# Two-layer decoder kernel: routing work of the last attention spread over four groups, range clears of semaphores, and two loads moved to GpSimd's queue

## The reference, cut to what matters

```python
x = ln(x + attn0(x)); x = ln(x + xattn0(x, ctx)); x = ln(x + soft_moe(x))
x = ln(x + attn1(x)); x = ln(x + xattn1(x, ctx)); x = ln(x + block(x))
def block(x):                                   # the last stage, with an attention of its own
    x = x + attention(layernorm(x, ln1_g, ln1_b))          # causal, 16 heads
    flat = layernorm(x, ln2_g, ln2_b)                      # 2048 tokens, 256 wide
    logits = flat @ gate_W + gate_b                        # 8 experts
    top_v, top_i = top_k(logits, 2); w = softmax(top_v)
    return x + sum over the 2 chosen experts e of w_e * (gelu(flat @ W1[e] + b1[e]) @ W2[e] + b2[e])
```

## Time and profile before

| | us |
|---|---|
| median of 3 runs (2824.33 to 2837.35) | 2835.46 |
| the profiled execution | 2807.25 |
| its span | 2805.4 |
| PE busy | 2516.5 (90%) |
| DVE busy | 1493.9 (53%) |
| ACT busy | 1326.3 (47%) |
| POOL busy | 452.0 (16%) |

### The profile page before, as it was taken

One profiled execution on the slowest core, in us unless ns is written; L12 is line 12 of the kernel. 1 busy time (PEld: TensorE's weight loads), 2 busy tenths in 40 slices (PEclk: granted clock), 3 DMA queues, 4 the chain that ended last, 5 costly groups with the idle time before them and its releaser, 6 DMA issues. The chain is left out here.

```text
span 2805.4 us, 47501 instructions
## 1 busy us (share of the span) xinstructions
PE 2516.5 (90%) x15751; PEld 1441.7 (51%) x15752; DVE 1493.9 (53%) x4204; ACT 1326.3 (47%) x2826; POOL 452.0 (16%) x730
## 2 busy tenths in 40 slices
PE   6999999999979889999699999999998998499991
PEld 3555544444434456676365544444445555267761
DVE  2555777788644500023455588878756565222224
ACT  3655466677754421111255556766675444122220
POOL 4233212101100000000113322112122123200004
PEclk8999999999999999999799999999999888699995
DMA  7555534232700022103644452332322445211103
GB/s 226 159 141 145 134 96 104 53 80 69 251 1 1 1 96 95 65 21 138 180 133 140 138 131 66 83 102 67 101 76 80 136 144 197 74 32 32 34 30 96
DMA packets 158432, 276.79 MB, mean 99 GB/s; under 512 B 22928, under 2 KB 101008, under 8 KB 153744
## 3 DMA queue, kind: packets, MB, share of 16 engines
q1 hardware_dynamic: 155152, 265.71, 33.1%
q0 software_dynamic: 3072, 8.39, 0.9%
HBM read 195.51 MB, written 95.29 MB: 104 GB/s over the span
## 5 line engine op out<-in xcount | busy, mean ns | idle before, releaser
L1626 ACT ACTIVATE second_p<-psum 128x512 f32<-128x512 f32 (+3 forms) x1024 | 462.2, 521 | 262.0 <-PE psum L1427 258.4
L1626 ACT ACTIVATE first_p<-psum 128x512 f32<-128x512 f32 (+3 forms) x768 | 366.6, 549 | 166.0 <-PE psum L1427 162.6
L1724 DVE TENSOR_REDUCE second_max_parts<-psum 128x1 f32<-128x512 f32 x512 | 322.5, 682 | 67.1 <-PE psum L1404 63.7
L1724 DVE TENSOR_REDUCE first_max_parts<-psum 128x1 f32<-128x512 f32 x512 | 322.5, 682 | 64.9 <-PE psum L1404 63.6
L1720 DVE CUSTOM_DVE_ANT_0 second_masked<-psum,mask_qk 128x384 f32<-128x384 f32 (+3 forms) x512 | 229.4, 488 | 196.4 <-PE psum L1404 173.9
L1439 PE MATMUL psum<-second_p,second_v_aug 128*32 128x512 f32 (+3 forms) x2048 | 237.9, 537 | 5.7 <-ACT second_p L1626 4.8
L1417 PE MATMUL psum<-second_q,second_k 64*128 64x512 f32 (+3 forms) x1024 | 226.5, 438 | 9.7 <-DVE second_max_parts L1720 6.8
L1404 PE MATMUL psum<-second_k,second_q 64*128 64x512 f32 (+3 forms) x1024 | 200.8, 389 | 26.3 <-DMA second_k<-a_k_parts 13.7
L1427 PE MATMUL psum<-second_shift_T,choose 64*128 64x512 f32 (+3 forms) x1024 | 199.5, 384 | 0.0
L1417 PEld LDWEIGHTS psum<-second_q,second_k 64*128 64x128 f32 x1024 | 98.5, 188 | 190.6 <-ACT second_p L1626 76.3
L1439 PE MATMUL psum<-first_p,first_v_aug 128*32 128x512 f32 (+3 forms) x1536 | 185.4, 554 | 1.1 <-ACT first_p L1626 0.7
(11 more groups left out here) (339 smaller groups left out, 3740.1 us busy)
## 6 DMA issues: line engine op xcount, KB each, us to landing
first_k<-c_k_parts SPq DMA_DIRECT2D x64, 256.0 KB, 4.8
second_q<-a_q_parts SPq DMA_DIRECT2D x128, 128.0 KB, 2.9
second_k<-a_k_parts SPq DMA_DIRECT2D x128, 128.0 KB, 2.9
second_k<-c_k_parts SPq DMA_DIRECT2D x64, 256.0 KB, 4.9
first_q<-a_q_parts SPq DMA_DIRECT2D x64, 128.0 KB, 3.2
first_k<-a_k_parts SPq DMA_DIRECT2D x64, 128.0 KB, 3.2
c_k_parts<-first_held SPq DMA_DIRECT2D x16, 512.0 KB, 3.2
first_q<-c_q_parts SPq DMA_DIRECT2D x64, 128.0 KB, 4.2
```

The lines of the kernel that those rows point to most:

```text
L1626: evacuated(act.activation(probs[tile % 2][:, 2 * h + p, q0:SEQ], bank[:, q0:SEQ], ACT.Exp, scale=scale), event)
L1724: evacuated(v.reduce_max(max_parts[n % 2][:, h, p, qt, k0 // BANK:k0 // BANK + 1], bank[:, 0:width], axis=AX_X), event)
```

## The change

Four edits:

1. `Core.stage` sorts the numbers of the stage's semaphores and clears each run of consecutive numbers with one instruction.
2. The routing pieces of a2. They are cut finer (`gate_scale` and `gate_add` a tile at a time, `gate_top` in four parts, `gate_place` in three), and for b = 0 and 1 they lie in four groups in place of three: in group first+1 only the output and the statistics; in first+2 aggregate, root, a pause and scale; in first+3 add, a pause, turn, a pause and logits; in first+4 top, a pause and rank; in first+5 place and send. For b = 2 everything ends in group 47 as before, with the rows in 46 and logits to send in 47. For b = 3 it all comes behind the last group, as before.
3. The four gate loads leave the "weights" event and come in a new event at the start of group 4.
4. In the routed stage the down bias and the residual are issued by POOL; the residual only when DVE has read two results. DVE waits for the down bias at the first result.

```diff
                 @block.gpsimd
                 def _(pool):
-                    for sem in self.stage_sems:
-                        pool.sem_clear(sem)
+                    numbers = sorted(sem.num for sem in self.stage_sems)
+                    for _, run in itertools.groupby(enumerate(numbers), lambda x: x[1] - x[0]):
+                        run = [number for _, number in run]
+                        pool.sem_clear(range(run[0], run[-1] + 1))
...
-        pieces += [("gate_stats", slot, 1), ("gate_aggregate", slot, 0), ("gate_root", slot, 0), ("gate_scale", slot, 0)]
+        pieces += [("gate_stats", slot, 1)]
...
+    measure = [("gate_aggregate", slot, 0), ("gate_root", slot, 0)]
+    scale = [("gate_scale", slot, t) for t in range(QT)]
+    add = [("gate_add", slot, t) for t in range(QT)]
+    turn = [("gate_turn", slot, k) for k in range(DK)]
+    top = [("gate_top", slot, part) for part in range(4)]
+    place = [("gate_place", slot, part) for part in range(3)] + [("gate_send", slot, 0)]
+    return measure, scale, add, turn, [("gate_logits", slot, 0)], top, [("gate_rank", slot, 0)], place
...
-                        if gate:
-                            fetch_weights(gate_loads, gate_in)
+                    elif event[0] == "gate_weights":
+                        fetch_weights(gate_loads, gate_in)
...
                 load(tile_at(0, 0, 0))
...
-                sp.dma_start(down_bias[:, :, :].rearrange("p e d -> p (e d)"),
-                             a["L1_ffn_exp_b2"].rearrange("e d -> (e d)").partition_broadcast(P)).then_inc(down_bias_in, 16)
-                for b in range(BATCH):
-                    sp.dma_start(residual[:, b * QT:(b + 1) * QT, :], block_in[b].rearrange("(q p) d -> p q d", p=P)
-                                 ).then_inc(residual_in, 16)
...
                         e = weights_of(v, t)
+                        v.wait_ge(down_bias_in, 16)
...
-                v.wait_ge(down_bias_in, 16)
                 for_steps(v, body)
...
             @block.gpsimd
             def _(pool):
+                pool.dma_start(down_bias[:, :, :].rearrange("p e d -> p (e d)"),
+                               a["L1_ffn_exp_b2"].rearrange("e d -> (e d)").partition_broadcast(P)).then_inc(down_bias_in, 16)
+                pool.wait_ge(y_read, 2)
+                for b in range(BATCH):
+                    pool.dma_start(residual[:, b * QT:(b + 1) * QT, :], block_in[b].rearrange("(q p) d -> p q d", p=P)
+                                   ).then_inc(residual_in, 16)
                 pool.wait_ge(residual_in, 16 * BATCH)
...
-            turned, best, ranked, placed = gate_pieces(slot)
-            if b < BATCH - 1:
+            measure, scale, add, turn, logits, top, rank, place = gate_pieces(slot)
+            if b < BATCH - 2:
                 pieces[first + 1] = pieces.get(first + 1, []) + output_pieces(a2, slot)
-                pieces[first + 2] = [REST] + turned
-                pieces[first + 3] = best + [REST] + ranked + [REST] + placed
+                pieces[first + 2] = measure + [REST] + scale
+                pieces[first + 3] = add + [REST] + turn + [REST] + logits
+                pieces[first + 4] = top + [REST] + rank
+                pieces[first + 5] = place
+            elif b < BATCH - 1:
+                pieces[first + 1] = pieces.get(first + 1, []) + output_pieces(a2, slot) + measure
+                pieces[first + 2] = scale + [REST] + add + [REST] + turn
+                pieces[first + 3] = logits + top + [REST] + rank + place
             else:
-                pieces[first] = output_pieces(a2, slot) + turned + best + ranked + placed
+                pieces[first] = output_pieces(a2, slot) + measure + scale + add + turn + logits + top + rank + place
+        contexts[GROUPS] = [("gate_weights", 0, 0)]
```

More of the change, by code:

```diff
@@ L14 @@
+import itertools
 import math
@@ L1877, in gate_scale, with gate_add @@
                     wait_for(v, gate_sent, 16 * 2 * QT * b)
[L1878 to L1882, removed]
+                    gate_do(v.scalar_tensor_tensor(rows[:, t, :], x_of(slot)[:, t, :], g_mean_var[:, t, 0:1], gate_gain[:, :],
+                                                   ALU.subtract, ALU.mult), wait=t == QT - 1)
+                def gate_add(event):
+                    _, slot, t = event
                     b = slot % BATCH
-                    if b == BATCH - 1:
+                    if b < BATCH - 1:
+                        v.wait_ge(gate_inverted, b + 1)
+                    elif t == 0:
                         v.wait_ge(gate_rooted, 1)
                         gate_do(v.reciprocal(g_rstd[:, :], g_root[:, :]))
[L1887 to L1891, removed]
+                    v.scalar_tensor_tensor(rows[:, t, :], rows[:, t, :], g_rstd[:, t:t + 1], gate_shift[:, :],
+                                           ALU.mult, ALU.add).then_inc(gate_rows, 1)
                 def logits_read(event):
@@ L1905, in gate_top @@
                 def gate_top(event):
-                    _, slot, _ = event
+                    _, slot, part = event
                     b = slot % BATCH
                     tiles = slice(b * QT, (b + 1) * QT)
[L1909 to L1927, removed]
+                    if part == 0:
+                        wait_evacuated(v, ("gate_logits", slot, 0))
+                        for t in range(QT):
+                            gate_do(v.max(top[:, t, :], logits[:, t, :]), wait=t == QT - 1)
+                    elif part == 1:
+                        for t in range(QT):
+                            gate_do(v.max_index(top_at[:, t, :], top[:, t, :], logits[:, t, :]), wait=t == QT - 1)
+                    elif part == 2:
+                        gate_do(v.tensor_tensor(lead[:, tiles], top[:, :, 1], top[:, :, 0], ALU.subtract), wait=False)
+                        gate_do(v.tensor_copy(top_f[:, :, :], top_at[:, :, :]))
+                        v.wait_ge(gate_numbers, NUMBERS)
+                        for x in range(2):
+                            gate_do(v.tensor_tensor(pick[x][:, tiles, :], number[:, 0:E].unsqueeze(1).to_broadcast([P, QT, E]),
+                                                    top_f[:, :, x:x + 1].to_broadcast([P, QT, E]), ALU.is_equal), wait=x == 1)
+                    else:
+                        gate_do(v.tensor_tensor(both[:, tiles, :], pick[0][:, tiles, :], pick[1][:, tiles, :], ALU.add))
+                        for t in range(b * QT, (b + 1) * QT):
+                            ins = v.tensor_tensor(earlier[:, t + 1, :], earlier[:, t, :], both[:, t, :], ALU.add)
+                            if t == (b + 1) * QT - 1:
+                                ins.then_inc(gate_masked, 1)
+                                v.wait_ge(gate_masked, b + 1)
+                            else:
+                                gate_do(ins)
@@ L1929, in gate_place @@
                 def gate_place(event):
-                    _, slot, _ = event
+                    _, slot, x = event
                     b = slot % BATCH
                     tiles = slice(b * QT, (b + 1) * QT)
-                    wait_evacuated(v, ("gate_rank", slot, 0))
-                    for x in range(2):
+                    if x < 2:
+                        wait_evacuated(v, ("gate_rank", slot, 0))
                         gate_do(v.tensor_tensor(picked[:, :, :], pick[x][:, tiles, :], rank_at[:, :, :], ALU.mult))
```

12 lines of the change are left out of this document (6 added, 6 removed).

## The result

The changed kernel takes 2784.7 us (median of 4, 2784.1 to 2791.9) against 2833.6 before: ratio 0.984, interval 0.982 to 0.985. The forecast was 2793. The profiled execution is the one of 2784.09, with a span of 2782.3; that of before took 2807.25. So the two profiled executions lie 23 us apart and the medians 49, and a good part of what follows is about this difference.

What follows compares the result with a forecast made beforehand. PE, busy 90% of the span, was taken as the bound, with time lost to its waits, low clock and stage ends. 13.6 + 19.6 + 1.9 + 7.5 - 0.5 = 42.1 us off the 2835.46 median gave 2793 us, range 2780 to 2808.

Steps and rivals of the forecast that it cites:

- clears: Stage ends: 172 fewer clear instructions at 0.079 us each, all on the path; 13.6 us gained, bounds 0 and 13.6.
- a2: Head groups with routing pieces: fewer waits and the clock staying up; 19.6 us gained, bounds 5 and 28.
- context: Start of "second": the context's load issued earlier, ahead of four gate loads; 1.9 us gained, bounds 0 and 3.
- routed start: Routed stage: tile 1's load issued earlier, so the first up product starts earlier; 7.5 us gained, bounds 5 and 9.
- residual: Routed stage: the residual's 2 MB come while tiles 2 to 4 run; 0.5 us lost, bounds 0 and 8.
- sum: Whole kernel: gains at stage ends, head groups, context and routed start less the residual's loss; 42.1 us gained.
- rival 2: Stage ends: a range clear costs per semaphore, so nothing is gained there; time 2807 us, chance 0.08.
- the prediction's own signs: Wrong if PEclk stays under 0.9 in groups 38 to 44, stage ends take 3 us, or PE waits for row loads.
- rival 1: Head groups: waits move and the clock falls all the same; 4.3 us gained instead of 19.6, time 2808, chance 0.15.
- Queues: Gate loads, down bias and residual moved: 1.9 at the context, 7.5 at the routed start, 0.5 lost to the residual.
- rival 3: Routed stage: row loads land behind the residual, 2.7 us late for three tiles, 8 us; time 2801, chance 0.06.
- the prediction's signs of being wrong: PEclk under 0.9 in groups 38 to 44, stage ends of 3 us, PE waiting for row loads of tiles 2 to 5.

Runs made afterwards that it cites:

- e10: Changed kernel with the logits product of b = 0 and 1 in two halves of 8 matmuls, in groups 39/40 and 43/44; 2788.8 us, 0.9841 of before.
- e8: Changed kernel with routing pieces of b = 0 and 1 set by step, logits halved, rank a step behind top, residual loads two tiles apart; 2789.9 us, 0.9847 of before.
- e6: Changed kernel without the sends of b = 0 and 1, their rows not written; 2771.8 us, 0.9860 of before.
- e4: Changed kernel with place and the eight sends of b = 0 and 1 at the end of groups 40 and 44; 2773.4 us, 0.9865 of before.
- e7: Changed kernel with scale, add, transposes and halved logits of b = 0 and 1 set by hand into their group's four steps; 2782.1 us, 0.9890 of before.

## Why the forecast came out near, step by step

| step | forecast | measured |
|---|---|---|
| clears | 13.6 | 11.9 in the traces, 11.6 alone |
| a2 | 19.6 | 27 with stops; about 15 without |
| context | 1.9 | 2.6 in the first two traces; about 1.7 over all |
| routed start | 7.5 | 6.2 (14.85 to 8.70) |
| residual | -0.5 | -1.0 and -2.4 |
| sum | 42.1 | 49 with stops |

**Clears.** The mechanism was right and rival 2 fell: a range costs by the instruction, with a little by its length (90 ns in the middle, 289 for 48). The price was 0.074 and not 0.079, and the ten new ones cost 1.4.

**a2.** Groups 38 and 42 near 12, 39 and 43 near 17 (16.95, 15.37), the longest unit wait 1.5 and none for the add: all as forecast. Wrong was that the clock stays up. Behind the wait of 1.55 for the unit in group 39 came 3.4 us of 1.2 GHz. The same wait of 1.55 stands in group 43, and no low clock follows it there (15.37 us at 0.98), so the wait alone doesn't decide it. And 40 and 44, which I took at little over the plain 11.56, take 14.02 at 0.79. That fall stands behind no wait but behind the logits product, 1.95 us of sixteen matmuls 8 columns wide. Where the product is cut in halves the clock stays up: groups 40 and 44 are at 1.00 and 1.00 in e10, at 1.00 and 0.97 in e8. How long the fall lasts isn't explained by this: it is 6.8 us in the changed kernel, but 3.4 in e6, with the same product in the same place (group 40 takes 12.65 us there). By the prediction's own signs this part was wrong: PEclk is under 0.9 in groups 39, 40, 41 and 44. So rival 1 was right in its "falls all the same" and wrong in its size: falls of 3.4 and 6.8 us cost 1.6 and 2.5, where groups 38 and 42 lost 9.1 and 10.1 before. Without stops groups 32 to 47 take 257.5 before and 241.6 in e4, 15.9, less 1.2 behind group 47 (43.6 to 44.8 us from there to the clears, of which I had 1): about 15 instead of 19.6, or 17 if the scatter of group 36 is left out. With stops they go from 290.2 to 257.9, 32 us, less 2.4 behind group 47; alone the pieces brought 27, and the other 3 us are not followed up.

The Trainium skill, "TensorE: Matmul & The Clock Gate", section "A second HAM failure mode: psum-queue depth-cycling", lets the clock swing on small idle times. The trace agrees in part: the wait of 1.55 us is followed by low clock in group 39 and not in group 43, and the fall at the start of group 40 stands behind no idle time.

**Queues.** 1.9 + 7.5 - 0.5 = 8.9 forecast, 9 measured (6 to 12), so this sum is right within the interval only; the first two traces give 2.6 + 6.2 - 2.4 = 6.4. PE's wait for the context fell from 9.19 to 6.60 us there, but it scatters: 8.3 to 9.3 in the four traces with the old order of loads, 6.1 to 9.2 in the ten with the new one, 8.9 and 7.2 on average. The routed start gained 1.3 less than forecast: tile 0's transposes began 5.1 us after the issue of its load and tile 1's 4.8 us after theirs, where I had 3.5 for the landing beside the down bias. The 2 MB of residual did delay row loads (one landed after 6.4 us instead of 2.0), as rival 3 said, but for two tiles and by 2.4 us at most. That PE waits for the row load of tile 4 is the second of the prediction's signs of being wrong that came. The rule of "DMA: Bandwidth & Descriptors", section "Queues, rings and completion order" in the Trainium skill, that a semaphore waits for its engine's earlier writes in all queues, agrees with that 6.4.

**The step that failed** is the one ahead of the sum: "The median of the runs shown lies 28 us above that execution, for no reason that the trace can show; taken off the median the forecast is 2793". There was a reason, and it touched the change: by their times most executions had stops beside the very sends that it moves (only the profiled ones can be looked into). The change took away some of their price: groups 40, 41, 44 and 45 together take 82.1 us in the second trace of before and 79.5 in the changed kernel's first, though the new ones hold the top and rank besides, and 46 and 47 fell from 30.2 to 19.6. That the forecast landed within 9 us is luck in part: the sum of 42.1 was made for a kernel without stops, where e4 gained 38 (0.9865 of 2811), and was taken off a median with stops, where the gain was 49. It lies between the two since a2 was forecast 3 to 5 us too high for the first case. Against its own kind, taken off the 2811.2 of the set without stops, the forecast would have been 2769; e4 took 2773.

## What to carry to other kernels

When the profiled execution lies a per cent under the median, as here, the trace may show another case than the times: ask for a second trace before a sum is taken off the median. Look for low clock behind work too, and not only behind waits: the product 8 columns wide was followed by it here, and its halves with other work between them were not. Laying DVE's work into more groups paid, where one block of it held up PE; cutting it finer inside the groups (e7, e8) only moved the wait to the next hand-over. One pair of traces is too little for a term of 1 or 2 us: the wait for the context and group 36 scatter by 3 us.

## What was not expected of the hardware

- **Stops.** Beside eight indirect sends in a row, one every 1.27 us (128 KB each), PE, ACT and DVE stand idle at once for 1.0 to 4.7 us. All traces of two sets have such stops beside the sends of b = 0 and 1, and so has the first one of the changed kernel; the first trace of before and those of the second set have none. The first stop begins 4.1 to 10.7 us after the first send, and the last one ends between 1.8 us before and 2.7 us after the issue of the last send. In the 12 us from the first send of a burst on, the traces with stops hold 46 to 83 records of semaphore updates, the ones without 176 to 325. The cause stays open. The Trainium skill, "NOTIFIC — the notification-queue block", section "7.1 Overflow: three behaviours, one of which stalls the engine", says that where a queue of such records is full the block, by its setting, either loses records or holds up what produces them. Here engines stand and update records are missing at once, which one setting on one queue doesn't give. No run separates this from the sends' own traffic. Every execution here, timed ones too, has a granted clock on record and so was recorded, and no run tells whether one that isn't recorded stops. Whether spreading the sends helps where there are stops was not tried.
- **Range clears.** 44 ns for one semaphore, 289 ns for 48 in one instruction, 3.37 us for 48 in 48.
- **Low clock without a wait.** 6.8 us at 1.2 GHz behind sixteen matmuls of 8 columns (3.4 in e6), none with eight and eight (e8, e10).
